# Window attention: one maximum over four score banks per half chunk, in place of one over two banks for each half unit

## The reference

```
x = x + conv(ln_c(x))        # conv: instance norm, qkv, attention in 8 x 8 windows, projection
t = tokens(x)
t = t + ffn(ln_t(t))         # ffn: softmax router over 8 experts, the best 2, weighted sum
```

```
attn = softmax(einsum('...qd,...kd->...qk', qw, kw) * scale, axis=-1)
out  = einsum('...qk,...kd->...qd', attn, vw)
```

## Time and profile before

| | us |
|---|---|
| median of 3 runs | 525.16 (524.7 to 525.29) |
| the profiled execution, its time | 523.7 |
| its span (first to last instruction) | 522.0 |
| one chunk of the loop, 14 of them alike | 16.51 |

### The profile page before, as it was taken

How to read it: one execution, slowest core, us unless ns; L and a number is a source line. 1 busy time by engine, 2 the same in 40 slices (tenths; PEclk the granted TensorE clock), 3 DMA queues, 4 the chain that set the end, 5 groups by cost and what they waited for, 6 DMA issues and landing times.

```text
span 522.0 us, 12739 instructions
## 1 busy us (share of the span) xinstructions
PE 427.4 (82%) x4882; PEld 233.9 (45%) x4882; DVE 410.2 (79%) x575; ACT 244.4 (47%) x409; POOL 79.9 (15%) x88
## 2 busy tenths in 40 slices
PE   4796799999999999999999989746959878668773
PEld 1232266666666666666666655312424323112210
DVE  0488877888888888888889887586799899899553
ACT  2653376565665656666566567061612532112110
POOL 6810000000000000000000000000422522453532
PEclk9999899999999999999999999896999989988888
DMA  8300000000000000000000000093208536556551
GB/s 315 142 0 1 1 3 1 3 0 0 0 0 0 0 0 0 0 0 0 0 0 0 0 1 3 17 205 76 57 21 186 158 91 162 149 121 155 154 145 41
DMA packets 10901, 28.80 MB, mean 55 GB/s; under 512 B 3200, under 2 KB 4736, under 8 KB 10496
## 3 DMA queue, kind: packets, MB, share of 16 engines
q1 hardware_dynamic: 8400, 20.46, 15.4%
q0 software_dynamic: 2048, 6.29, 3.9%
q10 hardware_dynamic: 432, 1.77, 0.9%
HBM read 5.96 MB, written 4.19 MB: 19 GB/s over the span
## 4 chain that ended last, share of the span: by engine, by line
PE 51%; DVE 23%; issue 9%; ACT 6%; SPq 5%; DMA 2%; DVEq 1%; POOL 1%; ACTq 0%; POOLq 0%
PE psum L445 9%; PE psum L462 9%; PE psum L305 5%; PE psum L430 4%; PE psum L587 4%; SPq L206 4%; PE psum L406 3%; PE psum L401 3%; DVE window_work L913 3%; DVE neg_max L910 3%; PE psum L325 3%; PE psum L471 3%; PE psum L579 2%; PE psum L557 2%; DVE o_tok L921 2%
## 5 line engine op out<-in xcount | busy, mean ns | idle before, releaser
L715 ACT ACTIVATE probs<-psum 128x512 f32<-128x512 f32 x128 | 76.0, 595 | 51.2 <-PE psum L445 50.8
L445 PE MATMUL psum<-weights_sb,window_work 128*128 128x128 f32 x512 | 82.0, 283 | 4.2 <-DVE window_work L913 4.2
L913 DVE TENSOR_TENSOR window_work<-psum,neg_max 128x1024 f32<-128x1024 f32 x64 | 78.4, 1225 | 7.2
L462 PE MATMUL psum<-probs,v_cols 128*32 128x64 f32 x2048 | 82.4, 223 | 0.2 <-DVE o_tok L921 0.2
L910 DVE TENSOR_REDUCE neg_max<-psum 128x16 f32<-128x1024 f32 x64 | 77.3, 1208 | 3.1 <-PE psum L430 3.1
L445 PEld LDWEIGHTS psum<-weights_sb,window_work 128*128 128x128 f32 x512 | 58.3, 142 | 47.4 <-issue 39.6
L256 POOL TENSOR_TENSOR window_work<-stage,q_sb 128x512 f32<-128x512 f32 x16 | 20.6, 1290 | 364.1 <-ACT q_sb L806 354.5
L462 PEld LDWEIGHTS psum<-probs,v_cols 128*32 128x32 f32 x2048 | 61.7, 110 | 23.8 <-issue 20.9
L579 PE MATMUL psum<-gate_rows,gate_sel_sb 128*128 (+1 forms) x128 | 45.4, 407 | 13.1 <-DVE probs L1065 5.6
L430 PE MATMUL psum<-stage 32*64 32x256 f32 x1024 | 36.1, 389 | 15.6 <-ACT stage L699 12.8
L699 ACT ACTIVATE stage<-k_sb,weights_sb 128x512 f32<-128x512 f32 x64 | 45.7, 718 | 0.0
(11 more groups left out here) (95 smaller groups left out, 610.6 us busy)
## 6 DMA issues: line engine op xcount, KB each, us to landing
stage<-x_win SPq DMA_DIRECT2D x112, 128.0 KB, 2.6
out<-out_sb POOLq DMA_DIRECT2D x16, 256.0 KB, 2.5
stage<-in_x SPq DMA_DIRECT2D x3, 1024.0 KB, 14.3
stage<-x_win POOLq DMA_DIRECT2D x16, 128.0 KB, 3.3
gate_rows<-gate_parts SPq DMA_DIRECT2D x48, 32.0 KB, 1.8
stage<-in_x SPq DMA_DIRECT2D x2, 512.0 KB, 6.2
weights_sb<-weights ACTq DMA_DIRECT2D x1, 875.5 KB, 10.1
gate_f<-gate_sel ACTq DMA_DIRECT2D x1, 512.0 KB, 13.4
```

Source lines behind the costliest of these rows:

```text
L445: last = nc.tensor.transpose(bank[TURN_BANKS[v % 2]][:, k * P:k * P + P], shifted[:, unit % 2 * 2 + half_b, at:at + P], const["c_ident"][: ...
L462: last = nc.tensor.matmul(bank[OUT_BANK][C * b:C * b + C, at:at + TOK], v_cols[:, u, (win * IMG + b) * HALVES + hh, :, :, :].rearrange("p ...
L715: nc.scalar.activation(probs[:, w % 4, :], bank[TURN_BANKS[w % 2]][:, :], ACT.Exp).then_inc(exp_done, 1)
L913: nc.vector.tensor_tensor(shifted_unit[:, unit % 2, :, :], t, neg_max[:, unit, :].unsqueeze(2).to_broadcast([P, 2 * PAIRS * HEADS, TOK]), ...
```

## The change

One `tensor_reduce` of all four score banks, 2048 columns, is issued at the start of each half. The two shifts that follow are only the additions. The wait on `score_ps` stands before the reduce, and both shifts wait for it by `max_done`, which now counts two a chunk in place of four. `neg_max` has the same size and the same places for each unit. TensorE's, ScalarE's and the DMA queues' programs are the same as before.

```diff
+            def maximum(m, hf):
+
+                dve.wait_ge(score_ps, m * 2 + (hf + 1))
+                t = score_banks.rearrange("p b (g k) -> p b g k", k=TOK)
+                nc.vector.tensor_reduce(neg_max[:, 2 * hf:2 * hf + 2, :].rearrange("p u (b g) -> p (u b) g", b=2),
+                                        t, AX.X, ALU.max, negate=True).then_inc(max_done, 1)
+
             def shift(m, hf, ip):
 
-
                 unit = hf * 2 + ip
-                dve.wait_ge(score_ps, m * 2 + (hf + 1))
+                dve.wait_ge(max_done, m * 2 + (hf + 1))
+                dve.wait_ge(turned_ps, m * NW + (2 * unit - 2 + TURNED))
                 t = score_banks[:, 2 * ip:2 * ip + 2, :].rearrange("p b (g k) -> p (b g) k", k=TOK)
-                nc.vector.tensor_reduce(neg_max[:, unit, :], t, AX.X, ALU.max, negate=True).then_inc(max_done, 1)
-                dve.wait_ge(max_done, m * 4 + (unit + 1))
-                dve.wait_ge(turned_ps, m * NW + (2 * unit - 2 + TURNED))
                 nc.vector.tensor_tensor(shifted_unit[:, unit % 2, :, :], t,
                                         neg_max[:, unit, :].unsqueeze(2).to_broadcast([P, 2 * PAIRS * HEADS, TOK]),
                                         ALU.add).then_inc(shifted_done, 1)
...
             def chunk(m, first=False, final=False):
                 for hf in range(2):
+                    maximum(m, hf)
                     shift(m, hf, 0)
                     shift(m, hf, 1)
```

## The result

| | before | changed |
|---|---|---|
| median, us | 524.93 (519.74 to 525.29, 4 runs) | 546.61 (545.02 to 549.99, 4 runs) |
| ratio | | 1.0446, 95% interval 1.0362 to 1.0529 |
| profiled span, us | 522.0 | 544.1 |
| one chunk of the loop, us | 16.51 | 18.04 |

The ratio is that of the means; the medians are 4.1% apart, and one of the four runs before took 519.74 us, 5 us under the other three.

A forecast was written before the change was run, and what follows sets the result against it. It took the order between VectorE and TensorE as deciding, with no margin before turn 4. Late first shifts summed to 15.0 + 6.0 + 0.5 + 0.2 + 0.7 = 22.4 us, giving a 547.5 us median, range 545 to 551.

The forecast's parts named there:

- The chain: Chain that ended last: passes through VectorE at the first maximum of a second half, fourteen times 16.51 us apart.
- the 14 waits: TensorE's waits for a shift before turn 4 in second halves: 4.2 us in all, 0.30 each.
- the bounds of 1208 and 2416: Limits on the 2048-column reduce: no more than the present 1024-column one, or twice it; 2.28 us taken.
- The small terms: Chunk 0's second half 0.5 us; last chunk's first half 0.2 and second half 0.7.
- the two large ones: Late first shifts: 14 second halves at 1.07 us, 15.0; 13 first halves at 0.46, 6.0.
- about 0.4: New TensorE wait before turn 0 in first halves, expected some 13 times.
- What VectorE saves: Second shift of each half ends some 0.2 us earlier, 32 times, 7 us; worth nothing where VectorE then idles.
- Rival B: Between maximum and turn 4 in second halves: VectorE's throughput counts, saved 7 us come through, 518 us; chance 0.03.
- rival C: At the double reduce: it costs hardly more than the present one, so no change, 525 us; chance 0.03.
- rival A: At turn 0: first halves hide the lateness, only second halves pay, 16.4 us, 541.6 in all; chance 0.06.
- rival D: In the loop: TensorE's clock falls, 556 to 564 us, or the reduce doubles, 551.5; chance 0.10 together.
- the margin of 0.66: Slack in us between the shift of unit 0 and turn 0 in first halves, behind the keys' matmuls.

The follow-up runs named there:

- e2: Changed kernel with the one maximum over four banks in second halves only, first halves with two maxima as before: 539.72 us, 1.0271 of the kernel before.
- e4: Changed kernel with project issued ahead of turn 4 in chunks 1 to 14: 532.87 us, 1.0172 of the kernel before.
- e7: Kernel before plus a spare VectorE addition of 128 columns behind the second shift of every half: 524.54 us, ratio 0.9974.
- e1: Changed kernel with the one maximum over four banks in first halves only, second halves with two maxima: 531.63 us, 1.0121 of the kernel before.
- e5: Kernel before with project issued ahead of turn 4: 522.8 us, ratio 0.9920.
- e6: Kernel before with each shift split into two additions of 512 columns, so a turn waits only for the half it reads: 519.47 us, ratio 0.9872.
- e3: Changed kernel with two maxima of 1024 columns ahead of both shifts in place of the one of 2048: 549.74 us, 1.0457 of the kernel before.
- e8: e6 plus, on ScalarE, the last masked copy of the keys ahead of the exponential of turn 5: 518.07 us, 0.9835 of the kernel before.

## Why the prediction was right

- **The bound.** The chain and the 14 waits said that turn 4 had no margin. e2 and e4 show it: there each us of lateness costs one, and it costs less when TensorE has something else to do.
- **The price of the reduce.** 2.28 us expected from the slope of two rows, 2267 ns measured, between the bounds of 1208 and 2416. The estimate by the Trainium skill ("VectorE: DVE Perf Modes", "Side-by-side: where the cycles go for N=2048 bf16") was 2298, 1.4% over the measured value.
- **The sum, term by term.** From the scores of chunk 1 to those of the last chunk it took 251.97 us (74.64 to 326.61), before 231.00 (74.67 to 305.67): 20.97 more, against 15.0 + 6.0 = 21.0. Chunk 0, from its scores (57.78) to those of chunk 1, is 0.40 longer, expected 0.5. From the last chunk's scores to the first matmul of the spread deviations (L325), 24.39 in place of 23.80: 0.59, expected 0.9. The attention is 21.96 longer, forecast 22.4. In the last chunk's second half TensorE waited 0.54, not 0.7. The small terms, two of them taken between bounds, were 0.4 us too large in sum; the two large ones, 21.0 of 22.4 us, hold. The profiled execution went from 523.7 to 545.76 us, 22.1 more, and the median is 546.61 where 547.5 was forecast.
- **Period and waits.** 18.04 was forecast and is measured. Turn 4 waited 1.36 us (1.3 to 1.5), turn 0 0.25; the text had said "about 0.4" for the latter, which was the delay of the turn and not the idle in the trace. The turn now starts 206.12 - 204.74 = 1.38 us after the keys, before 195.48 - 194.51 = 0.97: 0.41 late, as worked out. The idle is counted only from the modelled end of the keys' matmuls, 1.12 us after their start.
- **What VectorE saves is worth nothing here.** e7 shows it with the opposite sign, and e1 and e2, which both save VectorE's time, are both slower. Rival B is refuted by them, rival C by the 2267 ns, rival A by e1's 0.47 us a chunk.
- **The clock** stayed at 1.00 in the loop, with idles of 1.36 us; rival D did not come. The stage ahead of the attention was 0.43 us shorter with the same program, and the later stages 0.57 us longer, at a granted clock of 0.87 in place of 0.91: 0.1 us in sum.
- **The noise** was taken too small. The prediction said that 0.2% can be told from none; the fourth run of the kernel before is 1% under the other three, and beside the experiments its runs lie between 522.04 and 528.01. The 22 us are far beyond that, but a difference like e5's 3 us isn't safe by the medians alone, and the small gains here are read from the periods.
- **The two rules** stood against each other as written: the Trainium skill ("Perfetto Trace Analysis", "Optimizing Scalar/DVE Operations") says that breaking up instructions may let work be completed sooner where an engine is not saturated but makes others wait. This case agrees: e6, with the smaller ones, is 1.3% faster. The 4.5% of the change are not the size of its instruction but the place of the second maximum, as e3 shows.

## What to carry to other kernels

Before merging two instructions of one engine, look at who waits for the first one's result, not at how much the engine saves: here some 0.2 us was saved a half and the first result came 1.07 us late. Read the margin at the waiting engine; a lateness cost here what went beyond it, once for each repeat (1.07 us of 1.07 in second halves; in first halves 0.47, of which 0.41 was beyond the margin of 0.66). Where the engine that is waited for has idle time of its own, smaller pieces with a signal each (e6) do what larger ones were meant to. When one wait is taken away, follow the waiting engine a few steps on before pricing the gain: e8 brought 0.13 us a chunk until the next wait was also moved.

## What was not expected of the hardware

A VectorE maximum over four PSUM banks, 2048 columns in one instruction, costs per column what it does over two: 2267 ns against 1208, a slope of 1.03 ns a column, the same as the 1.05 from 512 to 1024 columns. Two maxima of 1024 directly behind each other take 2.32 us from start to end in e3's timeline, less than 2 x 1208 = 2.42, since the second starts before the first has ended; so merging them saves 0.05 to 0.07 us and not the 0.15 that the two durations suggest. The group of e3's maxima shows the overlap: 64 of 1205 ns each would be 77.1 us, and they keep the engine busy for 74.6.

```profile
L909 DVE TENSOR_REDUCE neg_max<-psum 128x16 f32<-128x1024 f32 x64 | 74.6, 1205 | 3.1 <-PE psum L430 3.1
```
